# Convolution products made in pairs, with the fifth product of each on 64 rows of the array

## What is computed

```python
x = x + attention(_gn(x))      # over channels: 192 x 192 logits, softmax, output projection
x = x + deform(_gn(x))
# deform(v):
offset = clip(conv3x3(v, off_w, off_b), -8, 8)      # 18 channels
mask = 2 * sigmoid(conv3x3(v, mask_w, mask_b))      # 9 channels
# per tap k: sample v bilinearly at the pixel + tap + offset, times mask, then
out = einsum('bckhw,ock->bohw', p, w.reshape(co, c_, K)) + b
# batch normalisation over all images, gamma, beta, exact gelu
```

## Time and profile before

| | |
|---|---|
| median of 3 runs | 3922.26 us (3920.33 to 3923.71) |
| profiled execution | 3912.95 us |
| its span, first to last instruction | 3911.1 us |
| TensorE (PE) matmuls busy | 3499.2 us, 89% |
| PE weight loads (PEld) busy | 3042.3 us, 78% |
| VectorE (DVE) busy | 2563.2 us, 66% |
| ScalarE (ACT) busy | 2123.8 us, 54% |
| GpSimd (POOL) busy | 1479.6 us, 38% |

### The profile page before, as it was taken

One profiled execution on the slowest core, in us unless ns is written; L12 is line 12 of the kernel. 1 busy time (PEld: TensorE's weight loads), 2 busy tenths in 40 slices (PEclk: granted clock), 3 DMA queues, 4 the chain that ended last, 5 costly groups with the idle time before them and its releaser, 6 DMA issues.

```text
span 3911.1 us, 108686 instructions
## 1 busy us (share of the span) xinstructions
PE 3499.2 (89%) x38307; PEld 3042.3 (78%) x38307; DVE 2563.2 (66%) x5805; ACT 2123.8 (54%) x4790; POOL 1479.6 (38%) x1165
## 2 busy tenths in 40 slices
PE   3999999999999999999999999999999999999600
PEld 2788888888888888888888888888888888888600
DVE  3567766676677667666776676677666666776522
ACT  1556555565555555555555555555555655555422
POOL 1334433343444333434433343444343434443311
PEclk8999999999999999999999999999999999999855
DMA  2000010000001011100100010010001000110399
GB/s 65 20 10 29 29 29 21 29 29 27 12 29 29 22 29 29 29 10 29 29 29 21 29 29 29 11 29 29 21 29 29 29 15 23 29 29 10 108 363 320
DMA packets 50710, 169.91 MB, mean 43 GB/s; under 512 B 9664, under 2 KB 10880, under 8 KB 50176
## 3 DMA queue, kind: packets, MB, share of 16 engines
q1 hardware_dynamic: 39584, 136.75, 11.6%
q0 software_dynamic: 7168, 25.17, 1.6%
q10 hardware_dynamic: 3424, 0.90, 0.1%
HBM read 87.29 MB, written 75.50 MB: 42 GB/s over the span
## 4 chain that ended last, share of the span: by engine, by line
issue 37%; PE 36%; POOL 15%; DMA 4%; DVE 4%; ACT 2%; DVEq 1%; ACTq 1%; SPq 1%; POOLq 1%
POOL sT L1341 14%; PE sps L690 7%; PE acc L707 4%; PE acc L709 4%; PE acc L708 4%; DMA xn<-x_scratch 2%; PE zps L676 2%; PE zps L680 2%; PE zps L677 2%; PE zps L678 2%; PE zps L679 2%; DMA out<-x 1%; PE l L563 1%; DVE stats L994 1%; PE l L619 1%
## 5 line engine op out<-in xcount | busy, mean ns | idle before, releaser
L1341 POOL TENSOR_TENSOR sT<-ay,bx 128x768 f32<-128x768 f32 x768 | 1216.6, 1596 | 1037.1 <-PE sps L690 812.9
L1165 DVE TENSOR_TENSOR sl<-sps,sh 128x384 f16<-128x384 f32 x1536 | 847.1, 552 | 523.9 <-ACT sh L909 512.5
L707 PE MATMUL acc<-zh,sh 128*128 128x192 f16 x4608 | 1133.9, 246 | 0.3 <-ACT ypm L930 0.3
L709 PE MATMUL acc<-zh,sl 128*128 128x192 f16 x4608 | 1133.9, 246 | 0.0
L708 PE MATMUL acc<-zl,sh 128*128 128x192 f16 x4608 | 1133.9, 246 | 0.0
L909 ACT CAST sh<-sps 128x384 f16<-128x384 f32 x1536 | 737.7, 480 | 589.1 <-PE sps L690 579.8
L882 ACT CAST zh<-zps 128x288 f16<-128x288 f32 x1536 | 616.1, 401 | 694.0 <-PE zps L680 664.4
L1159 DVE TENSOR_TENSOR zl<-zps,zh 128x288 f16<-128x288 f32 x1536 | 696.0, 453 | 382.8 <-ACT zh L882 375.7
L690 PE MATMUL sps<-eye,sT 128*128 128x128 f32 x4608 | 773.6, 277 | 70.1 <-POOL sT L1341 64.6
L690 PEld LDWEIGHTS sps<-eye,sT 128*128 128x128 f32 x4608 | 541.6, 141 | 170.8 <-issue 114.2
L708 PEld LDWEIGHTS acc<-zl,sh 128*128 128x128 f16 x4608 | 451.0, 98 | 17.3
(11 more groups left out here) (202 smaller groups left out, 6366.8 us busy)
## 6 DMA issues: line engine op xcount, KB each, us to landing
xin<-in_x SPq DMA_DIRECT2D x32, 512.0 KB, 5.4
xin<-in_x SPq DMA_DIRECT2D x64, 256.0 KB, 6.0
x_scratch<-x SPq DMA_DIRECT2D x32, 512.0 KB, 2.7
y_scratch<-ych SPq DMA_DIRECT2D x32, 512.0 KB, 2.7
zh<-y_scratch SPq DMA_DIRECT2D x20, 512.0 KB, 10.6
zl<-x_scratch SPq DMA_DIRECT2D x20, 512.0 KB, 11.9
out<-zh POOLq DMA_DIRECT2D x20, 512.0 KB, 9.1
x_scratch<-x SPq DMA_DIRECT2D x32, 256.0 KB, 3.4
```

The lines of the kernel that those rows point to most:

```text
L707: pe.matmul(acc[:, 0:C], s_h, zh[:, j, ky, z], start=start and kx == 0, stop=False)
L709: mm = pe.matmul(acc[:, 0:C], s_l, zh[:, j, ky, z], start=False, stop=stop and kx == 2)
L1165: dve.tensor_tensor(one(sl), sps[u % S_BANKS][:, 0:3 * P], one(sh), ALU.subtract).then_inc(s_lo, 1)
L1341: pool.tensor_tensor(sT[:, p % ST_RING].rearrange("p k (r x) -> p k r x", r=R), a, x_, ALU.mult)\
```

## The change

The z groups are made two at a time, in every second unit. `z_pair(g)` makes g and g + 1, behind the splits of the pair before. First come the first four products of both groups, as before on 128 rows, and then the two fifth products, each on 64 rows: that of the first group takes the high part of the b channels from partitions 0 to 63 of x2_hilo_b, that of the second takes it from partitions 64 to 127 of a new tile `x2h` (and `x2wh` for tile 0). The product of the low part by the low weights falls away. ACT writes the high part of the b channels with two activations of 64 partitions, one into each tile, and DVE copies two more seams. The splits of both groups follow each other in ACT's and DVE's programs.

```diff
-                pe.matmul(o, at(0), wpr_h[:, 0, ky, n], start=True, stop=False)
-                pe.matmul(o, at(0), wpr_l[:, 0, ky, n], start=False, stop=False)
-                pe.matmul(o, at(1), wpr_h[:, 0, ky, n], start=False, stop=False)
-                pe.matmul(o, at(2), wpr_h[:, 1, ky, n], start=False, stop=False)
-                return pe.matmul(o, at(2), wpr_l[:, 1, ky, n], start=False, stop=True)
+                if g >= 2 or not first(b):
+                    pe.wait_ge(z_lo, UNITS * b + g)
...
+                hi_a, lo_a, hilo_b = (at(x2[k], x2w[k]) for k in range(3))
+                for i in range(2):
+                    o, n = zps[:, i, 0:KO // 2], slice(i * KO // 2, (i + 1) * KO // 2)
+                    pe.matmul(o, hi_a, wpr_h[:, 0, ky, n], start=True, stop=False)
+                    pe.matmul(o, hi_a, wpr_l[:, 0, ky, n], start=False, stop=False)
+                    pe.matmul(o, lo_a, wpr_h[:, 0, ky, n], start=False, stop=False)
+                    pe.matmul(o, hilo_b, wpr_h[:, 1, ky, n], start=False, stop=False)
+                for i, hi_b in enumerate((hilo_b[0:CB], at(x2h, x2wh)[CB:P])):
+                    o, n = zps[:, i, 0:KO // 2], slice(i * KO // 2, (i + 1) * KO // 2)
+                    pe.matmul(o, hi_b, wpr_l[i * CB:(i + 1) * CB, 1, ky, n], start=False, stop=True).then_inc(z_ps, 1)
...
-                    if u + AHEAD < UNITS:
-                        z_group(u + AHEAD, b, par)
-                    elif more:
-                        z_group(u + AHEAD - UNITS, b + 1, 1 - par)
+                    if u % 2 == 0 and u + AHEAD < UNITS:
+                        z_pair(u + AHEAD, b, par)
+                    elif u % 2 == 0 and more:
+                        z_pair(u + AHEAD - UNITS, b + 1, 1 - par)
...
+                if as_hi and n and i:
+                    for v, r in ((hi, slice(0, CB)), (inner(x2h, par), slice(CB, P))):
+                        ins = act.activation(v[r], src[r, i], ACT.Identity, scale=rstd[r, i:i + 1],
+                                             bias=nbias[r, i:i + 1])
+                    ins.then_inc(xn_hi, 1)
+                    return
...
+                    for g in (u + AHEAD, u + AHEAD + 1) if u % 2 == 0 else ():
+                        if g < UNITS:
+                            split_z(g, b, par)
+                        elif more:
+                            split_z(g - UNITS, b + 1, 1 - par)
...
+                if k == 2:
+                    high, edge = rows(inner(x2h, par)[CB:P]), rows(x2wh[CB:P, par])
+                    dve.tensor_copy(edge[:, 0:WRAP], high[:, H - WRAP:H])
+                    dve.tensor_copy(edge[:, WRAP:2 * WRAP], high[:, 0:WRAP])
...
-                    residue(1, inner(x2[2], par)[CB:P], inner(x2[2], par)[CB:P], 1, b)
+                    residue(1, inner(x2[2], par)[CB:P], inner(x2h, par)[CB:P], 1, b)
```

More of the change, by code:

```diff
@@ L155, in build @@
         x2 = [sb(f"x2_{n}", [P, 2, PAD_ROWS * W], F16) for n in ("hi_a", "lo_a", "hilo_b")]
+        x2h = sb("x2h", [P, 2, PAD_ROWS * W], F16)
+        x2wh = sb("x2wh", [P, 2, 2 * WRAP * W], F16)
         off = sb("off", [P, 2, TILES, J])
@@ L658, in part0, with z_pair @@
                         offset_conv(TILES // 2 * (u - 38) + t, b, par)
-            def z_group(g, b, par):
+            def z_pair(g, b, par):
                 if g == 0:
@@ L664, in z_group @@
                 if g >= 2 or not first(b):
-                    pe.wait_ge(z_lo, UNITS * b + g - 1)
-                z_product(g, par).then_inc(z_ps, 1)
-            def z_product(g, par):
+                    pe.wait_ge(z_lo, UNITS * b + g)
                 j, ky = tile_at(g // 6, par), g % 6 // 2
                 row = 4 * j + ky - 3 + PAD_T
[L672 to L675, removed]
-                pe.matmul(o, at(0), wpr_h[:, 0, ky, n], start=True, stop=False)
-                pe.matmul(o, at(0), wpr_l[:, 0, ky, n], start=False, stop=False)
-                pe.matmul(o, at(1), wpr_h[:, 0, ky, n], start=False, stop=False)
-                pe.matmul(o, at(2), wpr_h[:, 1, ky, n], start=False, stop=False)
-                return pe.matmul(o, at(2), wpr_l[:, 1, ky, n], start=False, stop=True)
+                at = lambda v, vw: vw[:, par, ky * W:(ky + ROWS_T) * W] if j == 0 else \
+                    v[:, par, row * W:(row + ROWS_T) * W]
+                hi_a, lo_a, hilo_b = (at(x2[k], x2w[k]) for k in range(3))
[8 more added lines that the diff above has]
+                    pe.matmul(o, hi_b, wpr_l[i * CB:(i + 1) * CB, 1, ky, n], start=False, stop=True).then_inc(z_ps, 1)
             def turn_s(u, b):
@@ L728, in far_image @@
                     part0(u, b + NB, 0, True)
-                for g in range(UNITS):
-                    z_group(g, b + NB, 0)
+                for g in range(0, UNITS, 2):
+                    z_pair(g, b + NB, 0)
                 pe.wait_ge(z_lo, UNITS * (b + NB) + UNITS)
@@ L757, in part1 @@
                 if first(b):
-                    for g in range(AHEAD):
-                        z_group(g, b, par)
+                    for g in range(0, AHEAD, 2):
+                        z_pair(g, b, par)
                     for u in range(S_BANKS):
@@ L801, in _, with normalize @@
             act.wait_ge(pool_setup, 1)
-            def normalize(as_hi, i, src, hi, n, b):
+            def normalize(as_hi, i, src, hi, n, b, par=0):
+                if as_hi and n and i:
[4 more added lines that the diff above has]
+                    return
                 if as_hi:
@@ L855, in part0 @@
                     i = (u - 30) // 2
-                    normalize(u % 2, i, x1, inner(x2[2 * i], par), 1, b)
+                    normalize(u % 2, i, x1, inner(x2[2 * i], par), 1, b, par)
                 if u == 41:
```

## The result

The changed kernel takes 4159.3 us (median, 4155.7 to 4163.3) against 3921.3 us before on the same chip: a ratio of 1.061, 95% interval 1.059 to 1.063. The forecast was 4065 us, range 3980 to 4165. So the sign holds and the time lies in the range, but at its upper end: +238 us where +143 was worked out. Of the kernels that follow, two had one execution each far above all their others (7374.8 us with pairs in odd units on 128 rows, 4464.1 us with the third pair at the tile's end), which is left out of their medians.

The account below looks back on a forecast made before the run. TensorE's full stream was taken as the bound. Overlap -75, shape changes +184, backlogs +28 and +6 gave +143 us: 3912.95 to 4056 us profiled, 4065 us with the runs' usual 9.3 us difference; range 3980 to 4165.

Parts of the forecast that it names:

- some 3 us of waits in an image: TensorE is busy 108.81 of 112.26 us an image; the remaining waits were taken as some 3 us an image.
- signs of being wrong: The prediction is wrong if an image takes under 112.2 us, or if most of the growth lies in waits.
- Part 1: Two fifth products on 64 rows run at once, starts 0.025 us apart: 0.0975 us saved a pair, -75 us.
- Part 2: Two changes of TensorE's array shape in each pair, 0.10 us into 64 rows and 0.14 out: +184 us.
- Part 3: Both splits of a pair follow each other on ACT and DVE: nothing in plain units, +28 and +6 us at two backlogs.
- rival C: The splits become a wait: cover gone in half the pairs, 0.3 us each, 115 us on top, 4180 us; chance 0.10.
- the room made for an fp32 load: Upper end of the range: up 77 us if the open load into 64 rows costs 0.11 in place of 0.01 us.
- Part 3 (a): Units 30 to 38: ACT's second activation and DVE's extra copies delay x2_moved, +0.9 us an image, 28 us; ends 0 and 1.5.
- (b): group_stats of unit 4: mv comes one zl (0.37 us) later, TensorE 0.16 later; +0.2 us an image, 6 us in all.
- A: Rival: the two halves of the array don't overlap, so nothing is saved there; 4140 us; chance 0.15.
- B: Rival: the array doesn't empty for these products, so the switch is free; about 3865 us; chance 0.12.

## Why the prediction was right, and where it was wrong

**What bounds the kernel** was right and carried the sign: TensorE's stream is full, so what is added to it is paid. But the "some 3 us of waits in an image" were read as a constant. The runs show waits that give way when TensorE slows down and grow when it speeds up: 36 of 92 us in the run on one half, some 80 of 348 us with single groups.

The prediction named its own signs of being wrong, and one of them came true: most of the growth lies in waits. In the balance above the stream has +85 us, while the rows from the tile ends to sT add up to +144 us. An image takes 119.5 us, where 116.7 were forecast. The right sign and a time inside the range thus don't mean that the mechanism was right: it accounts for about a third of the growth.

**Part 1** was too cautious: the starts are 0.003 apart, not the 0.025 us taken from the earlier trace rows; -92 in place of -75 us. The figure of the Trainium skill (TensorE: Matmul & The Clock Gate, Part 3), about 4 ns, agrees with the 3 ns of the trace. That this saving is there didn't decide anything.

**Part 2** was right step by step, on rows of another data type: 0.096 and 0.101 us where 0.09 to 0.10 was read from the earlier trace rows, the fp16 load open for practically nothing, the fp32 load for 0.055 us ahead of the transposes (0.165 us from the first to the second, 0.109 where the load is ahead). 177 in place of 184 us. The drain at a change of tiling mode that the Trainium skill states (TensorEngine Tiling (Array Packing), Key Properties) shows in every pair. Parts 1 and 2 together are +85 in the stream where +109 was forecast, and 53 to 73 us in the time, after waits and clock have moved too.

**Part 3** holds the failed step: "In plain units I cost this at nothing". It asked only whether the splits of a pair are ready for the next pair (they are: that wait grew from 5.4 to 10.0 us, so rival C didn't come). It didn't ask what the moved z group had been cover for. Of a tile's end the rule is in the code quoted ahead of the prediction: `convolve` of unit 6i waits for y_pm, and between the two stood turn_s and one z group, 0.94 us against 0.8 to 0.9 us that ACT needs. Taking 0.61 us away had to show: at five of the eight tile ends, 108 us. The same holds for the odd units 21 and 23 of the attention part, about 45 us for gram and mt_l. Unit 12 (about 11 us) is another case, since the pair still stands ahead of its transposes there: xhl_b itself comes later, with two zl ahead of it in unit 10 of DVE's program and with a longer operation of its own (last section). The ends given to part 3, 0 and 1.5 us an image, left it out as well; the range held the time only because of the room made for an fp32 load.

**Part 3 (a)** had about the size and the wrong place. TensorE waited less for x2_moved, not more (12.1 us in place of 20.5), since it had lost more ahead of that point; where x2h is left out and the gap before unit 36 is small, this wait is 40.0 us. x2h costs 48 us by itself and 17 us with pairs in the even units, against 28 forecast, through ACT's copy of acc in unit 36 behind it. **(b)**, mv, was right: +8 us against 6.

**Rivals.** A (no overlap) fell at the starts and by the run on one half. B (no emptying) fell at every pair. Neither C nor any other named the wait that took the largest part. That the sign was safe rests on parts 1 and 2. That the time fell into the range was luck: its upper end stood for an open load of 0.11 us that didn't come, and what filled it was a wait that no term had.

## What to carry to other kernels

Products on half of the rows pay only if many of them stand together: each change of shape costs 0.10 us of TensorE, plus the open load, and a pair of 288 columns has 0.12 us to win, so by these numbers it takes a run of at least two or three such pairs between two changes to gain (an estimate, not run). When work on the bounding engine is moved, list for every unit that it leaves which round trip of another engine (copy out of a bank, then release) it was standing over, with the length of both. And put a price on added waits and added stream separately: part of added stream comes back from waits. Then read the granted clock of both kernels before a difference in time is given to one cause: with the third pair at the tile's end the lower clock was more than half of it. Which pattern of waits brings the clock down wasn't taken apart here.

## What the hardware showed that was not expected

DVE and POOL lengthened each other's operations, and it is the one that starts second that gets longer. In the changed kernel DVE's low parts in units 8 and 10 mostly take 1.9 to 2.5 us in place of 1.22, and one bx of POOL's four in an image takes 2.14 us in place of 1.21, with the same shapes (the column after the count is busy us, then mean ns):

```profile
L1027 DVE TENSOR_TENSOR xhl_b<-xn,xhl_b 64x1024 f16<-64x1024 f32 x32 | 69.0, 2155 | 2.0 <-ACT xhl_b L813 1.0
L1338 POOL TENSOR_TENSOR bx<-off,cx_sb 128x576 f32<-128x576 f32 x128 | 185.6, 1450 | 577.0 <-DVE off L1135 577.0
```

Before, the means were 1222 and 1212 ns. One of the cases in the timeline of the changed kernel:

```profile
1952.48 2.02 DVE L1027 TENSOR_TENSOR xhl_b<-xn,xhl_b 64x1024 f16<-64x1024 f32 x1
...
1951.94 1.48 POOL L1354 TENSOR_TENSOR sT<-ay,bx 128x768 f32<-128x768 f32 x1 [2.23 <-PE sps L691]
1953.38 2.14 POOL L1338 TENSOR_TENSOR bx<-off,cx_sb 128x576 f32<-128x576 f32 x1
```

The starts and ends fit a simple order. DVE starts 0.54 us after sT and ends 1.08 us after sT has ended; bx starts meanwhile and ends 1.02 us after DVE has ended, as if each did its work only when the one ahead was through. All 54 of these DVE operations that start under an operation of POOL end 1.08 us after it (1.080 to 1.084). Before, DVE was first whenever the two met: it kept its 1.22 us, and it was POOL's sT, started 0.07 to 0.55 us later, that took 2.0 to 2.5 us in place of 1.48 and ended 1.34 us after DVE. This is part of why TensorE waits for xhl_b (19.9 us where 9.5 were). It is read from starts and ends only; no run took one of the two operations away.
